# VectorE takes the maximum of the attention scores ahead of collecting, with the one-hot compare between sum and maximum

## The reference, cut to what matters

```
feat = (h @ W).reshape(N, 4, 64)
el = einsum('nhd,hd->nh', feat, attn_l);  er = einsum('nhd,hd->nh', feat, attn_r)
e = leaky_relu(el[src] + er[dst], 0.2)
ex = exp(e - segment_max(e, dst)[dst])
alpha = ex / segment_sum(ex, dst)[dst]
rst = segment_sum(feat[src] * alpha[..., None], dst)
out = h + elu(rst + bias)
```

## Time and profile before

| | |
|---|---|
| median of three runs | 6529.58 us |
| the profiled execution: time | 6532.67 us |
| the profiled execution: span of the core | 6530.9 us |
| mean granted TensorE clock over the span | 0.904 |
| instructions | 127122 |
| walk, first to last `messages` | 1422.6 to 2960.7 us of the span |

### The profile page before, as it was taken

One profiled execution on the slowest core, in us unless ns is written; L12 is line 12 of the kernel. 1 busy time (PEld: TensorE's weight loads), 2 busy tenths in 40 slices (PEclk: granted clock), 3 DMA queues, 4 the chain that ended last, 5 costly groups with the idle time before them and its releaser, 6 DMA issues. The chain is left out here.

```text
span 6530.9 us, 127122 instructions
## 1 busy us (share of the span) xinstructions
PE 5098.4 (78%) x34156; PEld 4113.7 (63%) x34157; DVE 3381.7 (52%) x10342; ACT 2222.7 (34%) x6042; POOL 2219.6 (34%) x2057
## 2 busy tenths in 40 slices
PE   2665655428888888884797899999899997299997
PEld 1443332215555555554796688887788886299997
DVE  6898766528888888887455421113411114422222
ACT  0345666615555555556232300001200002433332
POOL 2577777765555555552221000000000000612221
PEclk8898777669999999995898999999999997599998
DMA  4478888875555555554565244442222223466665
GB/s 134 129 234 273 278 287 289 290 196 146 146 147 146 146 148 146 146 147 129 163 179 163 79 162 162 152 161 100 72 98 93 94 98 118 133 187 181 181 182 165
DMA packets 504762, 1057.75 MB, mean 162 GB/s; under 512 B 59670, under 2 KB 370317, under 8 KB 484972
## 3 DMA queue, kind: packets, MB, share of 16 engines
q1 hardware_dynamic: 385276, 706.86, 34.2%
q0 software_dynamic: 112144, 268.88, 15.0%
q10 hardware_dynamic: 7200, 80.28, 3.1%
HBM read 741.74 MB, written 323.21 MB: 163 GB/s over the span
## 5 line engine op out<-in xcount | busy, mean ns | idle before, releaser
L690 POOL DMA_INDIRECT arena<-table,arena x1664 | 1738.4, 1045 | 980.3 <-DVE arena L795 584.7
L1303 PE MATMUL banks<-arena 128*128 128x256 bf16 x14700 | 1623.7, 273 | 24.7 <-DMA arena<-counts 24.7
L1303 PEld LDWEIGHTS banks<-arena 128*128 128x128 f16 x14700 | 1439.5, 98 | 205.0 <-DMA arena<-counts 25.5
L869 PE MATMUL banks<-arena 128*128 128x261 f32 x3328 | 1009.5, 428 | 192.2 <-DVE arena L807 125.1
L620 PE MATMUL banks<-arena 128*128 128x392 bf16 x2368 | 602.2, 408 | 414.2 <-ACT banks L648 226.5
L2026 POOL DMA_INDIRECT expert_in<-arena,slot x147 | 161.2, 1097 | 2158.1 <-DVEq L1971 2116.4
L869 PEld LDWEIGHTS banks<-arena 128*128 128x128 f32 x3328 | 596.7, 199 | 330.5 <-DVE arena L807 134.0
L620 PEld LDWEIGHTS banks<-arena 128*128 128x128 bf16 x2368 | 338.2, 149 | 677.7 <-issue 635.4
L1357 DVE TENSOR_TENSOR rings<-rings,banks 128x256 f32<-128x256 f32 x98 | 41.3, 422 | 1344.1 <-PE banks L1295 1344.1
L2209 ACT ACTIVATE rings<-banks,b_sb 128x128 f32<-128x128 f32 x1296 | 370.5, 369 | 828.3 <-PE banks L2242 828.3
L795 DVE TENSOR_TENSOR arena<-arena 128x512 f32<-128x512 f32 x832 | 575.3, 692 | 141.4 <-ACT arena L742 140.4
(11 more groups left out here) (344 smaller groups left out, 5444.0 us busy)
## 6 DMA issues: line engine op xcount, KB each, us to landing
arena<-counts SPq DMA_DIRECT2D x100, 1568.0 KB, 6.7
arena<-in_L_ffn_W SPq DMA_DIRECT2D x114, 1024.0 KB, 5.2
edge_rows<-arena SPq DMA_DIRECT2D x416, 264.0 KB, 3.3
arena<-edge_rows SPq DMA_DIRECT2D x416, 264.0 KB, 2.9
counts<-arena ACTq DMA_DIRECT2D x50, 1568.0 KB, 6.8
arena<-in_L_ffn_w SPq DMA_DIRECT2D x64, 1024.0 KB, 5.2
expert_in<-arena SPq DMA_DIRECT2D x25, 2028.0 KB
arena<-table,arena POOLq DMA_INDIRECT x1664, 3.9
```

The lines of the kernel that those rows point to most:

```text
L690: pool.indirect_dma_start(out=got[:, u, j, :], out_offset=None, in_=table0, in_offset=bass.IndirectOffsetOnAxis(ap=src_sb[:, 2 * pair + j: ...
L869: last = pe.matmul(banks_a[u][:, 0:mw], onehot[:, u, j, :], msg[:, u % RB, j, 0:mw], start=(j == 0), stop=(j == 1))
L1303: last = pe.matmul(psum[u][:, 0:D], a_ring[:, u, a, :], parts[:, a, k, :], start=(a == 0 and k == 0), stop=(a == NT - 1 and k == 2))
```

## The change

In each body of DVE's walk, `collect`(u) and `make_onehot`(u+5) change places around `score_max`(u+2). The new order is `score_sum`(u+2), `messages`(u+1), `score_left`(u+2), `make_onehot`(u+5), `score_max`(u+2), `collect`(u). No instruction is added or taken away, and the programs of the other engines are the same.

```
                                 if two:
                                     score_left(*two)
-                                collect(i, u, tile(u))
+                                if u + RB + 1 < UN or not final(i):
+                                    make_onehot(i + (u + RB + 1) // UN, (u + RB + 1) % UN)
                                 if two:
                                     score_max(*two)
-                                if u + RB + 1 < UN or not final(i):
-                                    make_onehot(i + (u + RB + 1) // UN, (u + RB + 1) % UN)
+                                collect(i, u, tile(u))
```

## The result

The changed kernel takes 6412.1 us (median of four runs, 6411.9 to 6415.4) against 6529.8 for the kernel before (a fourth run, of 6530.0, has joined its three): a ratio of 0.9821, 95% interval 0.9804 to 0.9838. It is 1.8% faster, and 6410 was forecast. The walk, first to last `messages`, went from 1538.1 us to 1420.3 (1423.7 to 2844.1), 117.8 less; the rest of the program differs by 2.5 us between the two profiled executions. The total is nearly exact, but its terms were off both ways and cancelled.

A forecast was written before the change was run, and what follows sets the result against it. Rounds were taken as bound by DVE's 1.03 us before the maximum plus 0.675 latency over ACT. Savings 94 + 6 + 16 + 10 - 5 - 1 = 120 us gave 6410 us; 8-in-10 range 6388 to 6480.

The forecast's parts named there:

- The maximum moves forward: DVE's round: the maximum starts 0.90 us after `messages` instead of 1.03, so the latency-bound pitch falls from 1.705 to 1.575.
- The sequencer is held at the maximum: `collect`'s registers come after the maximum's release; `collect` at 1.10 us, `messages` free at 1.57, level with the path over ACT.
- ACT's path: Latency from maximum over ACT's exp to `messages`: 0.675 us, giving pitch 1.575 with the maximum 0.90 after `messages`.
- 720 rounds save 0.13: Rounds where `messages` waits for exp: 0.13 us saved in each of 720, 94 us.
- 94 + 6 - 5 - 1: Us saved: waiting rounds 94, first rounds of steps 6; lost: step starts 5, register groups up to 0.194 us 1.
- interplay with POOL: POOL's gathers, released by `messages`: two new rounds last 3.15 us against 2.3 needed per release, so they cost nothing.
- Half-clock steps: Steps with TensorE at half clock: 42 such steps, shorter for net 16 us; a third fewer, 10 us more saved.
- Step start 0.05 longer: Loop end comes 0.05 us later because the body's last instruction is `collect`, not one-hot: 103 times, 5 us lost.
- A: Rival: registers behind the maximum set the pitch; 0.1 us more there gives 1.65, about 6470 us; chance 0.15.
- D: Rival: the gain passes 2%; all half-clock steps gone, 19 us more saved, 6391 us; chance 0.07.
- C: Rival: slower; 0.55 us between the maximum's release and `collect` makes pitch 1.85, 6643 us; chance 0.04.
- B: Rival: no change; DVE's six full records, 1.92 us, are an order-independent floor, time 6530 us; chance 0.08.

The follow-up runs named there:

- one-hot first: The kernel before with only the one-hot moved, ahead of `collect` and the maximum: ratio to before 1.0169, walk 1668.0 us.
- maximum first: Against the kernel before, the maximum directly behind the left score, then `collect`, one-hot last: ratio to before 1.0074, walk 1591.5 us.
- wait pair: Changed kernel plus one always satisfied wait, either between maximum and `collect` (walk 1446.1 us) or in front of the one-hot (walk 1421.8 us).
- place ahead: Changed kernel with the tile's address, bounds stated, written to a register between sum and `messages`; `collect`'s waits stay: ratio to before 0.9817, walk 1417.5 us.
- the addition: Changed kernel plus one unused VectorE addition of 128x64 f32 between sum and `messages` in each round: ratio to before 0.9993, walk 1512.5 us.
- wait behind: Changed kernel plus one always satisfied wait between maximum and `collect`: ratio to before 0.9905, walk 1446.1 us.
- the assertions: Changed kernel with address in its own register and `collect`'s waits before the maximum; two range assertions landed behind it: ratio to before 1.0151, walk 1630.8 us.
- the version with the shortest round: Against the kernel before: one-hot and left score ahead of `messages`, then address write, maximum, `collect`: ratio to before 1.0305, walk 1765.9 us.

## Why the prediction was right, and where it was not

- *The maximum moves forward by 0.13 and pulls the pitch to 1.575*: right. 1.57 in three places of eight, 1.61 to 1.63 in four; one-hot first and maximum first show that the position of both instructions is what counts, with pitches of 1.91 and 1.72 to 1.78 where 1.905 and 1.77 were expected.
- *The sequencer is held at the maximum, `collect` at 1.10, both paths level*: right. In the fourth and eighth round `collect` comes at 1.11 and the wait pair shows the register path as the binding one. In the sixth it comes at 1.06 and ACT's path binds, as it does in place ahead, at the same 1.57. (Groups of 180 ns or more stand in four places of eight, not in two.) The Trainium skill (Perfetto Trace Analysis, "DVE / Act Engine Instruction") has the sequencer read on past a waiting instruction. These runs disagree, since a satisfied wait behind the maximum costs 0.03, and ahead nothing.
- *720 rounds save 0.13*: a little too much. An undisturbed step went from 14.47 us (mean of 66) to 13.67 (mean of 100), step start included: 102 x 0.80 = 82 us, where 94 + 6 - 5 - 1 = 94 was forecast. By place, the fourth, sixth and eighth round saved 0.14 each, the second 0.21 (0.19 forecast), but the third, fifth and seventh only 0.09: 12 us less than forecast. These are the rounds with long records of the left score. The interplay with POOL was missed: I had called its cost nothing, and moving the gathers brought the three to 1.56 to 1.58.
- *Half-clock steps*: mis-sized too. I took 42 waits for the number of such steps, a third of them away for 10 us and 16 for the others being shorter, 26 together. In the kernel before, 36 disturbed steps took 34.7 us more than as many undisturbed ones; in the changed kernel two took 1.5 more. That is 33 of the 117.8 us; 3 lie in the first and the last step. The direction (PE closer together) is borne out by the addition: 25 stretches at the old pitch. The size is that of one chip: where the kernel before has fewer stretches, by the estimate above, the whole saving is 100 us.
- *Step start 0.05 longer*: a little too small, 2.50 against 2.41, 3 us more than forecast. It is 0.03 longer where the left score's record is short and 0.10 where it is long.
- *Rivals.* A is what the wait behind shows on a small scale, C what the assertions did (1.0151). B, the floor by whole records (the Trainium skill, VectorE: DVE Perf Modes, "The DRAIN you can't avoid"), falls for good with rounds of 1.42 against records that add up to 1.92. The same section adds that a next instruction that isn't held starts earlier; the rows agree with that, 0.60 behind a `messages` of 0.68. D came true for the clock, yet not for the time: 12 us are missing elsewhere, and the stretches gave 33 us where 26 + 19 was D's price for them.

So 6410 against 6412 is closer than the working deserves: 12 us too much in one term met 10 too little in the others.

## What to carry over

Between an instruction that releases another engine and the one that needs the answer, put work to cover the whole latency. Then look at what the sequencer still has to do behind a held wait: here 29 ns cost in full there and nothing under a long instruction. Count DVE's floor from start-to-start distances, not from records. And look at TensorE's granted clock after each such change: it gave 33 us here for nothing, on a chip where it had fallen 36 times before, and stood at half in every step of the version with the shortest round.

## What was not expected of the hardware

- A register load of two words holds a sequencer for 0.53 us and of four for 0.97.
- A memset of 128x64 f32 between two VectorE instructions lengthens the round by 0.02 us, an addition of the same size by 0.13: starts behind the memset are closer (`messages` 0.03 after it, the left score 0.54 after `messages` instead of 0.60).
- A VectorE addition of 128x16 sometimes takes 0.20 to 0.24 us instead of 0.17, and holds the next by 0.04 to 0.07 more. In the changed kernel all 305 such records start within 0.01 us of a POOL gather's start or 1.22 after one; but so do 105 short ones.
